# Column sums of a slot softmax taken with tokens on partitions, and its scales spread by one-pass matmuls

## The reference

```python
Pn = rmsnorm(P, input_norm_w); k_proj = Pn @ Wk.T; v_proj = Pn @ Wv.T      # P: 4 x 64 x 256
for _ in range(3):
    sn = rmsnorm(slots, slot_norm_w)                                       # slots: 4 x 1024 x 256
    scores = jnp.einsum('bkd,bmd->bkm', sn @ Wq.T, k_proj) * SCALE
    attn = jax.nn.softmax(scores, axis=-2)                 # over the 1024 tokens of a batch
    attn = attn / (jnp.sum(attn, axis=-1, keepdims=True) + EPS)            # over the 64 context rows
    updates = jnp.einsum('bkm,bmd->bkd', attn, v_proj)
    slots = gru_cell(updates, slots, gru_wih, gru_whh, gru_bih, gru_bhh)
```

## Time and profile before

| | us |
|---|---|
| median of 3 runs (lowest, highest) | 1280.48 (1280.4, 1283.75) |
| the profiled execution | 1288.91 |
| its span, first to last instruction | 1287.1 |
| setup, and what runs ahead of the loop | 0 to 93.1 |
| the six halves | 93.1 to 468 |
| gating and experts | 468 to the end |

### The profile page before, as it was taken

The page is one execution under the profiler, slowest core; times in us unless marked ns, Lnnn a source line. Parts: engine busy times, 40 slices in busy tenths (PEclk is TensorE's granted clock), DMA queues, the critical chain, the costliest instruction groups (busy, mean ns, idle before and its releaser), DMA issues. The chain is left out here.

```text
span 1287.1 us, 17969 instructions
## 1 busy us (share of the span) xinstructions
PE 1153.2 (90%) x6000; PEld 961.8 (75%) x6000; DVE 888.7 (69%) x1513; ACT 579.6 (45%) x866; POOL 415.8 (32%) x321
## 2 busy tenths in 40 slices
PE   5569989899999865899987799999999999999995
PEld 4446767676767754688876688888888888888884
DVE  7586888878778669677893566666666666666662
ACT  4244545454535426322343554545444544544441
POOL 4241333333310014233354123333333333332341
PEclk9659999998999987899989799999999999999998
DMA  4300000000000034300002544344444444444421
GB/s 150 87 8 10 9 9 9 8 5 11 0 17 9 9 131 132 106 17 33 17 33 82 206 114 123 99 117 127 126 131 131 131 104 110 123 127 127 131 34 17
DMA packets 45603, 95.58 MB, mean 74 GB/s; under 512 B 11008, under 2 KB 36864, under 8 KB 41216
## 3 DMA queue, kind: packets, MB, share of 16 engines
q1 hardware_dynamic: 31808, 75.98, 17.6%
q0 software_dynamic: 12288, 17.31, 8.0%
q10 hardware_dynamic: 1472, 1.84, 0.4%
HBM read 74.11 MB, written 17.07 MB: 71 GB/s over the span
## 5 line engine op out<-in xcount | busy, mean ns | idle before, releaser
L1863 DVE SCALAR_TENSOR_TENSOR ehid<-eup,b_up,esilu 128x512 f32<-128x512 f32 x128 | 96.1, 751 | 180.8 <-PE eup L1732 160.7
L1700 POOL DMA_INDIRECT out_tokens<-yo,idx_out x64 | 113.3, 1770 | 243.2 <-DVE yo L1837 228.6
L1786 ACT ACTIVATE esilu<-egate,b_gate 128x512 f32<-128x512 f32 x128 | 87.6, 685 | 154.5 <-PE egate L1732 153.5
L1745 PE MATMUL edown<-w_hi,eh_hi 128*128 128x256 f32 x512 | 145.3, 284 | 0.0
L1745 PE MATMUL edown<-w_hi,eh_lo 128*128 128x256 f32 x512 | 144.3, 282 | 0.0
L1745 PE MATMUL edown<-w_lo,eh_hi 128*128 128x256 f32 x512 | 143.0, 279 | 0.0
L1795 ACT ACTIVATE eh_hi<-ehid 128x512 fp32r<-128x512 f32 x128 | 81.0, 633 | 116.9 <-DVE ehid L1863 116.9
L1815 DVE TENSOR_TENSOR w_lo<-raw,w_hi 128x768 fp32r<-128x768 f32 x128 | 121.2, 949 | 7.8 <-ACT w_hi L1775 7.8
L522 PE MATMUL gate_banks<-slots_hi,whh_hi 128*128 128x512 f32 x288 | 119.4, 414 | 4.6 <-ACT tr L660 4.5
L522 PE MATMUL gate_banks<-slots_hi,whh_lo 128*128 128x512 f32 x288 | 116.6, 405 | 0.0
L522 PE MATMUL gate_banks<-slots_lo,whh_hi 128*128 128x512 f32 x288 | 116.3, 404 | 0.0
(11 more groups left out here) (278 smaller groups left out, 2743.0 us busy)
## 6 DMA issues: line engine op xcount, KB each, us to landing
raw<-in_w_expert SPq DMA_DIRECT2D x32, 1536.0 KB
token_rows<-work SPq DMA_DIRECT2D x8, 512.0 KB, 3.2
out_tokens<-y SPq DMA_DIRECT2D x8, 512.0 KB, 3.0
attn<-attn_lo SPq DMA_DIRECT2D x24, 128.0 KB, 2.3
work<-in_x SPq DMA_DIRECT2D x4, 512.0 KB, 4.9
raw<-in_x SPq DMA_DIRECT2D x4, 512.0 KB, 6.1
b_down<-in_down_b SPq DMA_DIRECT2D x1, 2048.0 KB, 7.2
raw<-in_w_shared SPq DMA_DIRECT2D x1, 1536.0 KB, 10.3
```

The lines of the kernel that those rows point to most:

```text
L1700: pool.indirect_dma_start(out, bass.IndirectOffsetOnAxis(idx_out[:, j:j + 1], 0), yo[:, j, :], None, compute_op=ALU.add).then_inc(g_add, 16)
L1745: last = nc.tensor.matmul(edown[:, j // 2, (j % 2) * D:(j % 2 + 1) * D], h[:, f % RING, tok], w[:, f, 4 * P:6 * P], start=(f == 0 and m == ...
L1786: nc.scalar.activation(esilu[:, f % 2, :], egate[:, f % 2, :], ACT.Silu, bias=b_gate[:, bass.ds(e, 1), f:f + 1].rearrange("p a b -> p (a b ...
L1863: nc.vector.scalar_tensor_tensor(ehid[:, f % 2, :], eup[:, f % 2, :], b_up[:, bass.ds(e, 1), f:f + 1].rearrange("p a b -> p (a b)"), esilu ...
```

## The change

1. `column_sums` now takes each block of 128 tokens of `expo` as the stationary operand and a 128 x 2 tile as the moving one: 8 matmuls of 2 columns. The sums come out with tokens on partitions, 128 x 16, in a corner of the bank `rms_b`.
2. DVE adds the epsilon, takes the reciprocal of 128 x 16, and splits it into a high part in columns 0 to 15 and a low part in columns 32 to 47 of `rec_parts` (`two_parts`). PE transposes them (`turn_rec`, inside unit (3,0)), DVE multiplies with `own_block`, now of 48 rows (`spread_reciprocal`, inside unit (3,0) behind `pre`), and PE spreads them with one one-pass matmul for each 512 tokens (`spread_rec`, behind unit (3,0)) into the `score` banks. `copy_csum` on ACT and the four long reciprocals on DVE go. `attention_half` reads the PSUM bank.
3. The token scales go the same way: `two_parts` behind `token_rms`, and `spread_rms` is a one-pass matmul.
4. `attention_lo` writes straight into the other 64 partitions of `attn`; `attn_lo` and the DMAs of `move_low` go.
5. ACT's first `attention_hi` and DVE's first `attention_lo` stand inside unit (3,1); `scores` waits for both `attention_half`s of the softmax before.
6. Setup: POOL makes masks of 48 rows (four more selects and a memset), ACT rounds `pick_group`; three more memsets stand at POOL's start of the loop's block.

```diff
-        own_block = asb("own_block", [GPP * BLK, BLK, P])
-        pick_group = asb("pick_group", [GPP * BLK, 2, P])
-        half_mask = asb("half_mask", [P, P])
+        NB = GPP * BLK
+        LOW = 32
+        NR = LOW + NB
+        own_block = asb("own_block", [NR, BLK, P])
+        pick_group = asb("pick_group", [P, 2, P], F32R)
+        batch_mask = asb("batch_mask", [P, 2])
...
+                act.wait_ge(c_pool, C_PICK)
+                for r in (0, LOW):
+                    nc.scalar.activation(pick_group[r:r + NB, :, :], pick_f[:, :, :], ACT.Copy)
...
-                n = 11
-                for j in range(GPP):
+                nc.gpsimd.memset(pick_group[:, :, :].bitcast(F32), 0.0).then_inc(c_pool, 1)
+                pool.wait_ge(c_pool, 12)
+                n = 12
+                for j in (*range(GPP), *range(LOW // BLK, LOW // BLK + GPP)):
...
-            csum_c = lsb("csum_c", [P, 2, GROUP])
             attn = lsb("attn", [P, PAIRS, 2, 2 * GROUP], F32R)
-            attn_lo = lsb("attn_lo", [P, GROUP], F32R)
-            spread = lsb("spread", [GPP * BLK, BLK, P])
-            rsum = lsb("rsum", [P, P])
+            spread = lsb("spread", [P, BLK, P], F32R)
+            rsum = lsb("rsum", [P, 2])
+            csum_e = lsb("csum_e", [P, NB])
+            rec = lsb("rec", [P, NB])
+            rms_parts = lsb("rms_parts", [P, P])
...
+            csum_t = rms_b[:, P:P + NB]
...
-                def move_low(s, pair, h):
-                    sp.wait_ge(v_alo, 2 * s + h + 1)
-                    for b in range(2):
-                        sp.dma_start(attn[rows_of(1 - b), pair, b, h * GROUP:(h + 1) * GROUP].bitcast(F32),
-                                     attn_lo[rows_of(b), :].bitcast(F32)).then_inc(d_alo, 16)
-                with sp.Fori(0, ITERS) as it:
-                    for pair in range(PAIRS):
-                        for h in range(2):
-                            move_low(2 * it + pair, pair, h)
-                sp.wait_ge(d_alo, 32 * 2 * PAIRS * ITERS)
...
-                        pe.wait_ge(d_alo, 32 * (4 * it + 2 * pair + g4 % 2 + 1))
+                        pe.wait_ge(v_alo, 4 * it + 2 * pair + g4 % 2 + 1)
...
-                def scores(s, pair, split_before):
+                def scores(s, pair, split_before, first=False):
+                    if not first:
+                        pe.wait_ge(v_attn, 2 * s)
...
                 def column_sums(s):
                     pe.wait_ge(v_rsum, s + 1)
+                    for c in range(2 * BLK):
+                        last = nc.tensor.matmul(csum_t.rearrange("p (b c) -> p b c", b=2)[:, :, c],
+                                                expo[:, c * P:(c + 1) * P], rsum[:, :], start=True, stop=True)
+                    last.then_inc(m_csum, 1)
+                def turn_rec(s):
+                    pe.wait_ge(v_recd, s + 1)
+                    nc.tensor.transpose(rms_b[:, 0:P], rec_parts[:, :], ident[:, :]).then_inc(m_rect, 1)
+                def spread_rec(s):
+                    pe.wait_ge(v_dia2, s + 1)
                     for h in range(2):
-                        nc.tensor.matmul(score[:, h, :], rsum[:, :], expo[:, h * GROUP:(h + 1) * GROUP],
-                                         start=True, stop=True).then_inc(m_csum, 1)
+                        nc.tensor.matmul(score[:, h, :], pick_group[:, h, :], spread[:, :, :].rearrange("p b t -> p (b t)"),
+                                         start=True, stop=True).then_inc(m_rec, 1)
...
-                    gru_unit(it, pair, 3, 0)
+                    gru_unit(it, pair, 3, 0, (lambda: turn_rec(s)) if softmax else None)
+                    if softmax:
+                        spread_rec(s)
                     gru_unit(it, pair, 3, 1)
...
-                def copy_csum(s):
-                    for h in range(2):
-                        act.wait_ge(m_csum, 2 * s + h + 1)
-                        nc.scalar.activation(csum_c[:, h, :], score[:, h, :], ACT.Identity,
-                                             bias=attn_eps[:, :]).then_inc(a_csum, 1)
...
                     gru_unit(it, pair, 2, 1)
-                    if softmax:
-                        copy_csum(s)
                     gru_unit(it, pair, 3, 0, high(pair, 2))
-                    if softmax:
-                        attention_hi(s, 1 - pair, 0)
-                    gru_unit(it, pair, 3, 1)
+                    gru_unit(it, pair, 3, 1, (lambda: attention_hi(s, 1 - pair, 0)) if softmax else None)
...
                     rsqrt_steps(nc.vector, do, rms[:, :], ms[:, :], rms_t[:, :])
+                    two_parts(s, rms_parts, rms, v_hi16, v_rmsd)
+                def two_parts(s, parts, full, v_high, v_done):
+                    high, low = parts[:, 0:NB].bitcast(F32R), parts[:, LOW:NR].bitcast(F32R)
+                    nc.vector.tensor_copy(high, full[:, :]).then_inc(v_high, 1)
+                    dve.wait_ge(v_high, s + 1)
+                    nc.vector.tensor_tensor(low, full[:, :], parts[:, 0:NB], ALU.subtract).then_inc(v_done, 1)
+                def own_columns(done):
+                    nc.vector.tensor_tensor(
+                        spread[0:NR, :, :], own_block[:, :, :],
+                        rms_b[0:NR, 0:P].rearrange("p (a q) -> p a q", a=1).to_broadcast([NR, BLK, P]),
+                        ALU.mult).then_inc(done, 1)
                 def spread_steps(s):
                     dve.wait_ge(m_rmst, s + 1)
-                    nc.vector.tensor_tensor(
-                        spread[:, :, :], own_block[:, :, :],
-                        rms_b[0:GPP * BLK, 0:P].rearrange("p (a q) -> p a q", a=1).to_broadcast([GPP * BLK, BLK, P]),
-                        ALU.mult).then_inc(v_diag, 1)
+                    own_columns(v_diag)
...
-                    nc.vector.tensor_scalar(rsum[:, :], half_mask[:, :], rden[:, :], None, ALU.mult).then_inc(v_rsum, 1)
+                    nc.vector.tensor_scalar(rsum[:, :], batch_mask[:, :], rden[:, :], None, ALU.mult).then_inc(v_rsum, 1)
...
-                def csum_reciprocal(s, h, part):
-                    dve.wait_ge(a_csum, 2 * s + h + 1)
-                    cols = slice(part * GROUP // 2, (part + 1) * GROUP // 2)
-                    nc.vector.reciprocal(csum_c[:, h, cols], csum_c[:, h, cols]).then_inc(v_rec, 1)
+                def csum_reciprocal(s):
+                    dve.wait_ge(m_csum, s + 1)
+                    nc.vector.tensor_scalar(csum_e[:, :], csum_t, ATTN_EPS, None, ALU.add).then_inc(v_rec, 1)
+                    dve.wait_ge(v_rec, 2 * s + 1)
+                    nc.vector.reciprocal(rec[:, :], csum_e[:, :]).then_inc(v_rec, 1)
+                    dve.wait_ge(v_rec, 2 * s + 2)
+                    two_parts(s, rec_parts, rec, v_rech, v_recd)
+                def spread_reciprocal(s):
+                    dve.wait_ge(m_rect, s + 1)
+                    own_columns(v_dia2)
                 def attention_half(s, h):
-                    dve.wait_ge(v_rec, 4 * s + 2 * h + 2)
-                    nc.vector.scalar_tensor_tensor(expo[:, half_of(h)], expo[:, half_of(h)], rden[:, :], csum_c[:, h, :],
+                    dve.wait_ge(m_rec, 2 * s + h + 1)
+                    nc.vector.scalar_tensor_tensor(expo[:, half_of(h)], expo[:, half_of(h)], rden[:, :], score[:, h, :],
                                                    ALU.mult, ALU.mult).then_inc(v_attn, 1)
-                def attention_lo(s, pair, h, first=False):
+                def attention_lo(s, pair, h):
                     dve.wait_ge(a_attn, 2 * s + h + 1)
-                    if not first:
-                        dve.wait_ge(d_alo, 32 * (2 * s + h))
                     for b in range(2):
-                        last = nc.vector.tensor_tensor(attn_lo[rows_of(b), :], expo[rows_of(b), half_of(h)],
+                        last = nc.vector.tensor_tensor(attn[rows_of(1 - b), pair, b, half_of(h)], expo[rows_of(b), half_of(h)],
                                                        attn[rows_of(b), pair, b, half_of(h)].bitcast(F32), ALU.subtract)
...
-                        csum_reciprocal(s, 0, 0)
-                        csum_reciprocal(s, 0, 1)
-                    gru_unit(it, pair, 3, 0, (lambda: attention_half(s, 0)) if softmax else None)
+                        csum_reciprocal(s)
+                    gru_unit(it, pair, 3, 0, (lambda: spread_reciprocal(s)) if softmax else None)
                     if softmax:
-                        attention_lo(s, 1 - pair, 0)
-                        csum_reciprocal(s, 1, 0)
-                    gru_unit(it, pair, 3, 1, (lambda: csum_reciprocal(s, 1, 1)) if softmax else None)
+                        attention_half(s, 0)
+                    gru_unit(it, pair, 3, 1, (lambda: attention_lo(s, 1 - pair, 0)) if softmax else None)
                     if softmax:
                         attention_half(s, 1)
...
+                dve.wait_ge(z_parts, 3)
...
-                csum_reciprocal(0, 0, 0)
-                csum_reciprocal(0, 0, 1)
```

(7 more changed lines are left out.)

39 lines of the change are left out of this document (23 added, 16 removed).

## The result

The changed kernel is slower: 1300.9 us (1299.73 to 1301.98, 4 runs) against 1282.12 (1280.4 to 1284.32, 4 runs), a ratio of 1.0146 with a 95% interval from 1.0127 to 1.0165. The forecast was 1275.3 with a range up to 1286.

A forecast was written before the change was run, and what follows sets the result against it. PE, busy 90% of the span, was taken as the bound, with a few holes. Terms -1.4 - 7.5 + 0.4 - 2.7 + 6.5 - 2.2 + 1.7 = -5.2 us took 1280.5 to 1275.3 us; range 1267 to 1286.

The forecast's parts named there:

- the clock: PE's granted clock in the loop: five falls costing 8 us after the change against 6.3 us before, +1.7 us.
- rival (d): The clock falls at every new hole or thin stretch, about 12 falls of 1.6 us: 1286 us, chance 0.12.
- The base: Whole kernel: the difference was taken off the median 1280.5 us, though the profiled execution took 1288.91.
- The new wait: PE behind unit (3,0) waits for DVE's `spread_reciprocal` before `spread_rec`: 2.7 us in each of five halves.
- The waits around it: Near unit (3,0), per half: the `rsum` wait shorter by 0.14 us; `turn_rec` and its possible wait, +0.25 us together.
- The transposition of the token scales: PE at `turn_rms`, about 23.8 us behind the half's start; -2.5 us in each of halves two to four, -7.5.
- Column sums: PE's `column_sums` in each half: eight two-record matmuls take 1.8 us against 1.82 before, so 0.
- DVE beside POOL: In the loop, POOL's square blocks the cast, the subtraction slips in, and `attention_half` falls from 2.55 to 0.7 us.
- Ahead of the loop: Before the loop, one-pass `spread_rms` and no second ACT copy let normalising start sooner: -1.4 us, bounds 0 and -2.1.
- (b): No clock falls at the new holes: two falls left, clock term -3.1 us, total 1270.5 us, chance 0.22.
- (c): DVE gains nothing up to `turn_rms`, as POOL may block it at the same places: 1284 us, chance 0.12.
- (e): In unit (3,0) the subtraction of `two_parts` is blocked, scales late for `turn_rec`: +4.6 us, 1280, chance 0.12.

The follow-up runs named there:

- the second profile: The kernel before, unchanged, profiled again: 1280.97 us (one run), with a loop of 369.8 us.
- early_spread: The changed kernel with VectorE's masked copy of the turned reciprocals made before its part of unit (3,0): 1281.6 us, ratio 0.9986 to the kernel before.
- low_in_place: The kernel before with only the low attention written in place by VectorE, without the DMA: 1294.78 us, ratio 1.0095.
- sums_after_r: late_turn with column sums in one block behind unit (3,0)'s r gate, reciprocals transposed behind its h gate and spread in unit (3,1): 1255.37 us.
- narrow_added: The kernel before with eight unread narrow matmuls (sixteen two-column records) added before the column sums in each of six places: 1305.52 us, ratio 1.0165.
- squares_moved: The changed kernel with the eight one-column sums of squares moved behind unit (3,0): 1293.65 us, ratio 1.0078 to the kernel before.
- late_turn: early_spread with the rms transposition after unit (1,0)'s h gate and its first spread after unit (1,1)'s r gate: 1266.86 us.
- filled_waits: early_spread with unread 512-column matmuls in two waits, eight before the rms transposition and four before the column sums: 1273.29 us.
- squares_joined: sums_after_r with the squares' sums moved right behind the column sums: 1257.18 us, ratio 0.9795 to the kernel before.
- one_pass: The kernel before with token scales as high and low rows spread in one pass, low attention still over its DMA: 1279.23 us.

## Why the prediction was wrong
**The step that failed is the clock**, "I take five falls, 8 us: +1.7". The trace shows 10 of the 14 waits of the changed loop followed by a fall: all four at the column sums, for 6.8 us each, and for 3.4 us four of five at the new wait, one of four at the token scales, and the sixth half's. Together these last 47.8 us (the 51.8 of the table hold 4.0 of stretches that begin ahead of the loop or at its very end). The term was 8 us; at half speed 47.8 us cost 23.9, less what of them lies in idle time. The forecast's own sign of being wrong, a granted clock below 0.93, is there in halves 2 to 4 (0.92). This is rival (d), given 0.12; its "from ten falls on" was the right point and its 1286 was still too low, since it priced each fall as one of 3.4 us and took off four falls of before, of which the second profile has one.

**The base was wrong too**: "a difference of the same work should hold for both". Most of the 6.3 us that the term took off for before's falls was not in the runs behind the median: the second profile has 8.0 us at low clock in the loop where the first has 23.4, and one fall within it, in the sixth half. With 1.6 for that one, the same sum, -6.9 + 8 - 1.6 = -0.5, gives 1280.0, no change, not faster.

**The rest of the sum stood, in part by luck.** In the loop the forecast is -5.5 us without the clock. Against the second profile the loop is 16.5 longer and has 43.8 us more at low clock, which at half speed is 21.9: 16.5 - 21.9 = -5.4. Halves 2 to 4 were forecast at 62.7 us at full clock: 67.8 less half of 10.2 us at low clock is 62.7. The first: forecast 65.7; 70.5 less half of the 10.2 that its two falls lasted is 65.4. The fifth: 57.5 forecast, 57.0 from the right start of that half in before, 58.5 less 1.7 is 56.8. The sixth: 56.1 to 53.9, the forecast -2.2. By its parts:
- *The new wait* was forecast at 2.7 in all five halves and is 2.42. Its reading of the order (the product behind the add that the unit's last matmul releases) was right, and early_spread takes it away by moving one instruction.
- *The waits around it* were not, and offset each other: the wait for `rsum`, 0.56 before, was to lose 0.14 and is 1.12; the 0.25 of waiting for the reciprocals' transposition didn't come, and the new wait is 0.3 shorter than forecast.
- *The transposition of the token scales* was forecast at 23.8 us behind the half's start: 187.70 less 163.9 is 23.8. Its first link was sized right too: the add of gate x was to start 8.6 us into the half and starts at 172.57, 8.7 in. low_in_place shows the forecast's remark on the DMA ("its removal gives nothing more in these halves") right in time and incomplete: it also joins two waits.
- *Column sums*, costed at 1.8: right at full clock (1.84 in sums_after_r), 2.63 in the changed kernel, where the clock is at 1.2 GHz from 209.90 on. narrow_added gives 22.6 us for 11 us of such matmuls.
- *DVE beside POOL*: the cast was to be blocked and the subtraction to slip in, and `attention_half` to take 0.7 for its 2.55. All three came, the third for a reason of its own (DVE and POOL in the second half):
```profile
213.26 1.89 POOL L965 TENSOR_TENSOR square<-slots 128x1024 f32<-128x1024 f32 x1 [6.66 <-DVE slots L805]
...
213.59 1.60 DVE L829 CAST rec_parts<-rec 128x16 fp32r<-128x16 f32 x1
215.22 0.18 DVE L831 TENSOR_TENSOR rec_parts<-rec,rec_parts 128x16 fp32r<-128x16 f32 x1
...
226.35 0.74 DVE L881 SCALAR_TENSOR_TENSOR expo<-expo,rden,score 128x512 f32<-128x512 f32 x1
```
The cast took 1.60 in the four halves in which POOL's square runs beside it and 0.17 in the fifth, where POOL is idle. The Trainium skill's lock of the port pair for a whole instruction ("SBUF — State Buffer", "Who interferes with whom") says the same, and the trace agrees: the cast ends at 215.19, 0.04 behind POOL's square.

The 0.74 of the first `attention_half` doesn't show that reading PSUM saves 1.8, as the forecast has it: POOL's `slots_lo`, which held it up before (215.99 to 218.40 beside the 2.55 from 216.40), is over at 224.43, two us ahead of it; and where POOL was idle, in the fifth half, it took 0.75 before too. The second `attention_half` does show something. In both kernels it starts 0.16 ahead of POOL's square; the square took 2.34 beside the one that reads two SBUF tiles and takes 1.90 beside the one that reads PSUM (before, then changed):
```profile
164.99 0.74 DVE L852 SCALAR_TENSOR_TENSOR expo<-expo,rden,csum_c 128x512 f32<-128x512 f32 x1
165.15 2.34 POOL L941 TENSOR_TENSOR square<-slots 128x1024 f32<-128x1024 f32 x1 [10.69 <-DVE slots L795]
...
168.55 0.74 DVE L881 SCALAR_TENSOR_TENSOR expo<-expo,rden,score 128x512 f32<-128x512 f32 x1
168.71 1.90 POOL L965 TENSOR_TENSOR square<-slots 128x1024 f32<-128x1024 f32 x1 [10.50 <-DVE slots L805]
```
- *Ahead of the loop* -1.4 is not seen; the loop starts at 93.4 (93.1 and 92.1 in the two profiles of before, 92.0 in squares_moved, whose work up to there is the same, so a us or two is scatter). ACT's normalising starts behind DVE's `shift`, not behind the copy that went, 1.1 earlier than in the first profile and 0.2 than in the second (71.88), where the forecast has 2.1:
```profile
71.66 2.07 ACT L754 ACTIVATE tr<-tr,shift,rstd 128x256 f32<-128x256 f32 x4 [5.49 <-DVE shift L941]
```

Of the other rivals, (b), given 0.22, was the furthest off, (c) is refuted by the 23.8, and (e) did not occur. The Trainium skill ("TensorE: Matmul & The Clock Gate", "HAM oscillation") describes a loop that idles in each pass and pays the slow start anew each time; the forecast weighed that lightly on the strength of three falls in eighteen. The page's example has waits of some 3 to 5 us, the changed kernel one of 3.2 and thirteen of 1.1 to 2.6. The traces bear the rule out in part: falls at ten of fourteen waits here, but none at the three waits of 2.3 us for the scales in halves 2 to 4, none behind early_spread's 2.6 us in the sixth half and none at late_turn's 0.9 us waits for the scales.

## What to carry to other kernels
Price a change of a loop twice, at full clock and by what its waits and narrow matmuls do to the granted clock: here the first was right to a us per half and the second was the whole verdict. A run of matmuls of one or two columns can be followed by a fall as a wait can (2.7 us of them were, in six of eight halves of filled_waits and squares_joined; 1.8 us of them alone were in none of four), so keep such a run short and away from waits. A short wait split in two by real work may be better than one in a single piece, though one_pass had falls with its waits apart. Before a base is corrected for something seen in one profile, profile it again.

## What the runs showed of the hardware
- A DMA and its wait taken away made the kernel 12 us slower (low_in_place): two waits of 1.7 to 1.8 us became one of 3.7 to 4.0, with 10.2 us at 1.2 GHz at it in each of three halves.
- 60 added matmuls of 512 columns in place of idle time made it 8.3 us faster (filled_waits against early_spread).
- The clock fell with TensorE idle for 0.3 us at most, behind sixteen records of two columns and eight of one (filled_waits, four of four halves).
- The same half of the same program has a fall in one execution and none in the next (the kernel before's third and fourth half), and that is worth 1.6 us each, though the fourth half's lasted 6.8 us: the wait for the scales behind it shrank from 1.83 us to 0.70.
- A VectorE cast of 128 x 16 that met GpSimd's square took 1.60 us for 0.17; and the square took 2.34 us for 1.90 when the VectorE instruction that had started 0.16 before it read two SBUF tiles and not one (changed kernel and before).
